# Ranks of r and c: one masked diagonal compare, and keys as columns from TensorE transposes

## The chip, the cores and the metric

One core of a Trainium2 chip. The metric is the device time of one execution in microseconds (us); lower is better.

## The reference

Two graph layers over 2708 nodes with 128 features, each followed by a residual and a layer norm. The first is a normalised diffusion plus softmax attention. The second is the one that the ranks serve:

```
XW = X @ W
s_col = XW @ a[0, :f];   s_row = XW @ a[0, f:]
Z1 = leaky_relu(s_row[:, None] + s_col[None, :], 0.01)
den = exp(Z1);  num = A @ den
att = where(num != 0, den / num, 0)
H = A @ (att @ XW)
```

The kernel calls `s_row` r and `s_col` c. It sorts the nodes by r and by c, so that for most pairs the sign of r + c (and with it the branch of the leaky relu) is known by tile, and the exponential splits into a product. For this it needs the rank of each r among all r, and of each c among all c.

## The kernel before, in words

The nodes are tiled in 22 tiles of 128 (the last has 20). Every engine has its own program; they meet at semaphores. Around the change five things run in one loop of 22 turns, one a tile `it`:

- TensorE (PE): `spread(it)`, 22 matmuls of the adjacency with the features of layer 0 (L1402); in every second turn the row transposes of a pair of tiles (L1415), in the others the products of a pair: r and c as rows over all partitions (L1425, into PSUM bank 7) and X W (L1429); then, from turn 7, `col_sums` of the rank steps of tile `it - 7`, one matmul of one column for each block (L1444).
- VectorE (DVE): the tail of tile `it` (L1030, L1033, and the two norm instructions L896, L898), then `rank_steps` of tile `it - 5`, for r (kind 0) and c (kind 1).
- ScalarE (ACT): the copies of the products (x1T L577, r and c into `rcb` L582, X W L587), then `row_sum` of the two steps of tile `it - 6` (L597).
- GpSimd (POOL): the layer norm of tile `it` (L415, L417, L423).
- SyncE: X W of each pair to DRAM.

After the loop come the rank steps of tiles 17 to 21: those of r, then (1, 17), (1, 18); then `settle(0)` turns r's ranks into positions, and steps (1, 19), (1, 20), (1, 21) stand between the works that follow it; then `settle(1)`.

A rank counts for each key the smaller ones. A step (kind, t) compares the 128 keys of tile t, as a column of per-partition scalars, with the keys of all tiles up to t, which lie as rows in `rcb`. In the version before it has three passes. First L920 takes the column out of the row: row times identity, summed over the row by the accumulator. Then L933 compares the blocks left of the diagonal with the column (`is_le`) into one of three wide buffers `Cb` (bf16), and L936 makes (equal) times the strict triangle mask U for the diagonal block. Last L942 adds (less) to that and sums it by rows with the accumulator. The wide buffer is summed by rows on ACT (`row_sum`, t blocks) and by columns on PE (`col_sums`, t blocks): a pair of different tiles is compared once and counted for both, as "less" on one side and as "not less" on the other. `settle` adds the row counts, the diagonal counts (`racc[kind][:, 1, :]`), the column sums and a constant `baseN`. A wide buffer is free for step n when the row sum and the column sums of step n - 3 are done. `Waiting` leaves out a wait that its engine has already met.

Of the kernel before, what the change touches and what calls it, by code (L numbers as in the profile page):

```python
# [5 lines left out]
P = 128  # L6
N = 2708
T = 22
# [75 lines left out]
def adj_resnorm2_kernel(nc, x, adjT, alpha, beta, W, a, rowk, out):  # L84
    with ExitStack() as ctx:
# [3 lines left out]
        def sem(name):  # L89
# [37 lines left out]
        tie = RF[:, 1664:1792].bitcast(BF16).rearrange("p (q j) -> p q j", q=2)  # L127
        junk = RF[:, 1792:1920].bitcast(BF16).rearrange("p (q j) -> p q j", q=2)
        racc = [RF[:, 1920 + 2 * T * q:1920 + 2 * T * (q + 1)].rearrange("p (q t) -> p q t", q=2) for q in range(2)]
# [75 lines left out]
        base = sq  # L205
# [31 lines left out]
        s_gset, s_rkset, s_ext, s_tie, s_less, s_diag, s_rowsum, s_rkmm, s_idx3, s_idxc = (  # L237
            sem(n) for n in ("s_gset", "s_rkset", "s_ext", "s_tie", "s_less", "s_diag", "s_rowsum", "s_rkmm",
                             "s_idx3", "s_idxc"))
# [44 lines left out]
        def less_no(n):  # L284

            return sum(t > 0 for _, t in STEPS[:n])
# [214 lines left out]
        def _(eng):  # L501
# [68 lines left out]
            def xw_part(part, g):  # L570
                t0, nb = PAIR[g]
                w, h = nb * P, g % 2
                if part == "rows":
                    av.wait_ge(s_x1T, g + 1)
                    if g >= 2:
                        av.wait_ge(s_xw, g - 1)
                    S.activation(x1T[h][:, 0:w], PSALL[:, 4, 0:w], ACT.Copy).then_inc(s_x1Tc, 1)  # L577
                else:
                    av.wait_ge(s_rc, g + 1)
                    av.wait_ge(s_xp, 12)  # L580
                    av.wait_ge(s_aoT, 6)
                    S.activation(rcb[:, :, t0 * P:t0 * P + w], PSALL[:, 7, :].rearrange("p (q n) -> p q n", q=2),  # L582
                                 ACT.Copy).then_inc(s_rcE, 1)
                    av.wait_ge(s_xw, g + 1)
                    if g >= 2:
                        av.wait_ge(s_XWd[h], 16 * (g // 2))
                    S.activation(XWb[h], PSALL[:, 4, 256:256 + w], ACT.Copy).then_inc(s_xwc, 1)  # L587

            def row_sum(kind, t):

                if t == 0:
                    return
                rows, m = rows_of(t), less_no(STEP[kind, t])
                av.wait_ge(s_less, m + 1)
# [27 lines left out]
            av.wait_ge(s_rkmm, less_no(len(STEPS)))  # L622
# [86 lines left out]
        def _(eng):  # L709
# [202 lines left out]
            def rank_steps(steps):  # L912

                for kind, t in steps:
                    n, rows, lo = STEP[kind, t], rows_of(t), t * P
                    dv.wait_ge(s_rcE, t // 2 + 1)
                    dv.wait_ge(s_const, CONST)
                    if n >= 2:
                        dv.wait_ge(s_ext, n - 1)
                    V.scalar_tensor_tensor(junk[:, n % 2, :], KEY[kind][0][:, lo:lo + P], 1.0, ident[:, :], ALU.mult,  # L920
                                           ALU.mult, accum_out=KEY[kind][1][:, t:t + 1]).then_inc(s_ext, 1)
                for kind, t in steps:
                    n, rows, lo = STEP[kind, t], rows_of(t), t * P
                    key, m = KEY[kind][0], less_no(STEP[kind, t])
                    sc1 = KEY[kind][1][0:rows, t:t + 1]
                    dv.wait_ge(s_ext, n + 1)
                    if t:
                        if m >= 3:
                            dv.wait_ge(s_rkmm, m - 2)
                            dv.wait_ge(s_rowsum, m - 2)  # L930
                        else:
                            dv.wait_ge(s_rsum, 1)
                        V.tensor_scalar(Cb[m % 3][0:rows, 0:lo], key[0:rows, 0:lo], sc1, None, ALU.is_le).then_inc(s_less, 1)  # L933
                    if n >= 2:
                        dv.wait_ge(s_diag, n - 1)
                    V.scalar_tensor_tensor(tie[0:rows, n % 2, 0:rows], key[0:rows, lo:lo + rows], sc1, U[0:rows, 0:rows],  # L936
                                           ALU.is_equal, ALU.mult).then_inc(s_tie, 1)
                for kind, t in steps:
                    n, rows, lo = STEP[kind, t], rows_of(t), t * P
                    dv.wait_ge(s_tie, n + 1)  # L940
                    dv.wait_ge(s_rkset, 2)
                    V.scalar_tensor_tensor(tie[0:rows, n % 2, 0:rows], KEY[kind][0][0:rows, lo:lo + rows],  # L942
                                           KEY[kind][1][0:rows, t:t + 1], tie[0:rows, n % 2, 0:rows], ALU.is_lt, ALU.add,
                                           accum_out=racc[kind][0:rows, 1, t:t + 1]).then_inc(s_diag, 1)

            def settle(kind):

                n = STEP[kind, T - 1]
                rank, x_, y_, hi_, lo_ = racc[kind][:, 0, :], wk[:, 0, :], wk[:, 1, :], wk[:, 2, :], wk[:, 3, :]
                dv.wait_ge(s_rkmm, less_no(n) + 1)  # L950
                dv.wait_ge(s_rowsum, less_no(n) + 1)
                dv.wait_ge(s_diag, n + 1)
                dv.wait_ge(s_dve2, base_ok)
                k1 = own.step(V.tensor_tensor(rank, rank, racc[kind][:, 1, :], ALU.add))
# [348 lines left out]
        def _(eng):  # L1303
# [102 lines left out]
            def xw_part(part, g):  # L1406
# [10 lines left out]
                else:  # L1417
                    pe.wait_ge(s_x1Tc, g + 1)
                    pe.wait_ge(s_wE, 3)
                    if g:  # L1420
                        pe.wait_ge(s_rcE, g)
                    else:
                        pe.wait_ge(s_ao, 11)
# [7 lines left out]
                    ins.then_inc(s_xw, 1)  # L1431

            def col_sums(kind, t):

                if t == 0:
                    return
                rows, m = rows_of(t), less_no(STEP[kind, t])
                pe.wait_ge(s_less, m + 1)
                if t == 1:
# [3 lines left out]
                for b in range(t):  # L1443
                    ins = TE.matmul(PSALL[:, 5 + kind, b:b + 1], Cb[m % 3][0:rows, b * P:(b + 1) * P],  # L1444
                                    ones[0:rows, :], start=False, stop=(t == T - 1 and b == t - 1))
# [238 lines left out]
```

## Time and profile before

| | |
|---|---|
| median of 3 runs | 751.45 us (749.09 to 752.02) |
| the profiled execution | 755.11 us, span 753.3 us |
| PE matmul busy | 629.9 us (84%), 4290 instructions |
| DVE busy | 598.8 us (79%), 1235 instructions |
| ACT busy | 449.8 us (60%), 693 instructions |
| POOL busy | 433.1 us (57%), 475 instructions |
| mean granted TensorE clock | 0.936 |

The loop with the ranks spans about 254 to 349 us of it, the steps of the last tiles up to about 395. Matmul records overlap, so that a duration there is longer than the step from one matmul to the next; where it matters the step is taken. In the timeline the number after x is how many instructions a row merges; "idle before" is how long the engine stood, and on what.

### The profile page before, as it was taken

The page shows a single profiled execution, that of the slowest core. Times are in us where ns is not written, and L with a number is a line of the kernel's source. Part 1 is how long each engine was busy: PE and PEld are TensorE (multiplying, and loading weights), DVE is VectorE, ACT ScalarE, POOL GpSimd, SP SyncE. Part 2 cuts the span into 40 slices and gives each one's busy share as a digit, 9 for nine tenths or more (in the row PEclk, how much of TensorE's full clock was granted, in tenths as well). Part 3 has the DMA queues.
Part 4 walks back from the last instruction along what each step waited for, and adds up shares of the span by engine and source line. Part 5 has one row for each costly group of instructions (what it writes and reads, how often), then busy time and mean ns, then how long its engine had stood idle before and what let it go on. Part 6 is the DMA issues. An engine that isn't in the chain of part 4 may idle for free.

```text
span 753.3 us, 12410 instructions
## 1 busy us (share of the span) xinstructions
PE 629.9 (84%) x4290; PEld 359.1 (48%) x4290; DVE 598.8 (79%) x1235; ACT 449.8 (60%) x693; POOL 433.1 (57%) x475
## 2 busy tenths in 40 slices
PE   5499999999996979986259879898999889886993
PEld 5243333333332969875235434444444444445882
DVE  2599999999998858999988578777788778786442
ACT  2388888888885504677840667666667667641000
POOL 5368888877777035776103257557588665201763
PEclk9999999999997689997559999999999999997997
DMA  9954444670000000000000234334334443200110
GB/s 143 103 58 40 38 41 40 148 289 1 1 1 4 2 8 22 16 15 16 7 1 19 74 85 126 98 105 121 88 101 120 122 115 91 84 4 2 31 29 16
DMA packets 19608, 45.65 MB, mean 61 GB/s; under 512 B 2922, under 2 KB 8574, under 8 KB 19486
## 3 DMA queue, kind: packets, MB, share of 16 engines
q0 software_dynamic: 9152, 31.95, 22.6%
q1 hardware_dynamic: 10334, 11.97, 4.9%
q8 instruction: 89, 1.46, 0.8%
q14 instruction: 33, 0.27, 0.1%
HBM read 56.34 MB, written 10.45 MB: 89 GB/s over the span
## 4 chain that ended last, share of the span: by engine, by line
PE 37%; DVE 30%; issue 16%; POOL 11%; ACT 3%; DMA 1%; DVEq 1%; POOLq 0%; ACTq 0%; SPq 0%
DVE ring L820 8%; PE PSALL L1636 7%; DVE R L829 7%; PE PSALL L1586 7%; POOL AW L454 6%; PE PSALL L1621 5%; PE PSALL L1402 4%; PE PSALL L1508 3%; PE PSALL L1383 2%; PE PSALL L1333 2%; DVE R L933 2%; PE PSALL L1588 2%; POOL X L445 1%; ACT XN L597 1%; PE PSALL L1457 1%
## 5 line engine op out<-in xcount | busy, mean ns | idle before, releaser
L392 POOL TENSOR_TENSOR R<-R,ring 128x452 f32<-128x452 f32 (+1 forms) x126 | 151.7, 1205 | 33.2 <-ACT ring L526 31.6
L454 POOL DMA_INDIRECT AW<-ATd,FR x66 | 90.3, 1367 | 79.0 <-DVE FR L1151 65.3
L829 DVE SCALAR_TENSOR_TENSOR R<-ring,R 128x452 bf16<-128x452 f32 (+1 forms) x132 | 134.8, 1022 | 0.0
L1586 PE MATMUL PSALL<-AW,R 128*128 128x452 fp8e4 (+1 forms) x540 | 124.3, 353 | 3.7 <-DVE R L1177 2.0
L1383 PE MATMUL PSALL<-R,AO 128*128 128x452 bf16 (+2 forms) x396 | 99.6, 361 | 16.1 <-DVE R L829 15.1
L526 ACT ACTIVATE ring<-ring,sm 128x452 f32<-128x452 f32 (+1 forms) x132 | 88.7, 672 | 27.5 <-DVE ring L820 20.9
L1333 PE MATMUL PSALL<-XN 128*128 128x452 f16 (+2 forms) x396 | 99.1, 361 | 4.7 <-issue 4.2
L534 ACT ACTIVATE R<-ring,sm 128x452 bf16<-128x452 f32 (+1 forms) x132 | 88.9, 673 | 4.3
L820 DVE TENSOR_TENSOR ring<-PSALL,AT 128x452 f32<-128x452 f32 (+1 forms) x132 | 81.0, 614 | 0.9 <-PE PSALL L1333 0.9
L1586 PEld LDWEIGHTS PSALL<-AW,R 128*128 128x128 bf16 x540 | 52.1, 97 | 56.4 <-issue 5.0
L1621 PE MATMUL PSALL<-ring,X 128*128 128x452 bf16 (+1 forms) x300 | 68.4, 362 | 12.6 <-issue 7.0
L690 ACT ACTIVATE TL<-PSALL,sm 128x452 f32<-128x452 f32 x66 | 42.0, 638 | 38.6 <-PE PSALL L1588 38.6
L1383 PEld LDWEIGHTS PSALL<-R,AO 128*128 128x128 bf16 (+1 forms) x396 | 28.4, 97 | 76.4 <-DVE R L829 62.5
L690 ACT ACTIVATE R<-PSALL,sm 128x452 f32<-128x452 f32 x66 | 42.1, 639 | 36.5 <-PE PSALL L1588 35.0
L1402 PE MATMUL PSALL<-R,AT 128*128 128x256 f16 x484 | 61.6, 288 | 0.0
L1243 DVE TENSOR_TENSOR ring<-ring 128x904 bf16<-128x904 f32 (+1 forms) x50 | 61.6, 1232 | 0.0
L1236 DVE SCALAR_TENSOR_TENSOR ring<-R,st,TL 128x904 f32<-128x904 f32 (+1 forms) x33 | 38.2, 1158 | 27.1 <-ACT TL L690 26.3
L1333 PEld LDWEIGHTS PSALL<-XN 128*128 128x128 f16 (+1 forms) x396 | 33.0, 97 | 51.7 <-DVE ring L820 28.5
L1636 PE MATMUL PSALL<-R,AT 128*128 128x256 f16 x484 | 55.3, 279 | 2.0 <-DVE R L1283 2.0
L445 POOL DMA_INDIRECT X<-XWd,idx x22 | 27.2, 1238 | 47.9 <-DVE idx L1017 41.7
L1636 PEld LDWEIGHTS PSALL<-R,AT 128*128 128x128 fp8e4 x484 | 48.4, 100 | 8.7 <-DVE R L1283 2.1
L1402 PEld LDWEIGHTS PSALL<-R,AT 128*128 128x128 fp8e4 x484 | 49.0, 103 | 7.5
(261 smaller groups left out, 1076.3 us busy)
## 6 DMA issues: line engine op xcount, KB each, us to landing
AT<-in_adjT POOLq DMA_DIRECT2D x22, 338.5 KB, 6.6
ATd<-AT SPq DMA_DIRECT2D x2, 3723.5 KB, 17.3
XWd<-ring SPq DMA_DIRECT2D x11, 128.0 KB, 1.8
out<-ring SPq DMA_DIRECT2D x21, 64.0 KB, 1.5
AW<-ATd,FR POOLq DMA_INDIRECT x66
X<-XWd,idx POOLq DMA_INDIRECT x22, 3.6
Wt<-in_W SPq DMA_DIRECT2D x1, 64.0 KB, 11.0
X<-in_x SPq DMA_DIRECT2D x1, 0.5 KB, 7.9
```

The costliest lines, as they stand in the source:

```text
L392: i = G.tensor_tensor(ES_, ES_, z, ALU.add)
L454: G.indirect_dma_start(out=AW2[:, jt % 3, q, :], out_offset=None, in_=ATd, in_offset=bass.IndirectOffsetOnAxis(ap=idxw[:, jt, q:q + 1], ax ...
L526: S.activation(z, z, ACT.Exp, scale=bcol[0:rows, :]).then_inc(s_exp, 1)
L534: S.activation(fh, z, ACT.Identity, bias=mone[0:rows, :]).then_inc(s_exp, 1)
L820: V.tensor_tensor(z, PSALL[0:rows, b, 0:w], A_, ALU.mult).then_inc(s_z, 1)
L829: V.scalar_tensor_tensor(F[0:rows, RW:RW + w], z, 1.0, F[0:rows, 0:w], ALU.subtract, ALU.subtract).then_inc(s_low, 1)
L1333: m = TE.matmul(PSALL[0:rows, b, 0:w], lh[:, jt * P:jt * P + rows], rh[:, c0:c0 + w], start=(k == 0), stop=(k == 2))
L1383: m = TE.matmul(PSALL[:, c, 0:w], half_[0:rows, jt, :], F[0:rows, o:o + w], start=(jt == 0 and k == 0), stop=(jt == T - 1 and k == 2))
L1402: ins = TE.matmul(PSALL[:, it % 4, 0:2 * D], AT[:, jt, it * P:(it + 1) * P], xp[:, jt, :, :].rearrange("p c d -> p (c d)"), start=(jt == 0 ...
L1586: TE.matmul(PSALL[:, b, 0:w], den_h[:, s + q, :, part], AW[:, jt % 3, q, c0:c0 + w], start=(q == 0 and part == 1), stop=False)
L1621: m = TE.matmul(PSALL[:, c, 0:CH[c][1]], XWh[:, jt, :, part], att[:, part_of], start=(jt == 0 and k == 0), stop=(jt == T - 1 and k == 2))
L1636: return TE.matmul(PSALL[:, out_bank[it], 0:2 * D], AT[:, jt, it * P:(it + 1) * P], xpY[:, jt, :, :].rearrange("p c d -> p (c d)"), start= ...
```

## The change

The diagonal block is written into the wide buffer beside the blocks left of it, as (`is_le`) times the mask U, by one instruction; L920, L936 and L942 with their buffers and semaphores go. Row sums and column sums take t + 1 blocks, also for t = 0. The diagonal is so counted as the other blocks are: its entries below the diagonal are compared once and serve both sides. `baseN` is changed to fit, and `settle` has no addition for the diagonal. The keys come as columns from TensorE: after the products of a pair PE waits for the copy of r and c (`s_rcE`), transposes four rows of one partition into columns of bank 7, and ACT copies them to `st` (`s_key`), before it goes on. The products of the next pair wait for `s_key` where they waited for `s_rcE`.

```diff
@@ setup (DVE) @@
-            k = own.step(V.tensor_copy(base, idx[:, 3, :]))
+            own.step(V.tensor_copy(base, idx[:, 3, :]))
             own.step(V.tensor_copy(pcol, idx[:, 0, 0:1]))
+            k = own.step(V.tensor_copy(baseN, idx[:, 0, :]))
             dv.wait_ge(s_dve2, k)
-            k = own.step(V.tensor_scalar(baseN, base, -1.0, float(N - P), ALU.mult, ALU.add))
-            dv.wait_ge(s_dve2, k)
-            k = own.step(V.tensor_copy(baseN[:, T - 1:T], idx[:, 0, T - 1:T]))
-            dv.wait_ge(s_dve2, k)
-            base_ok = own.step(V.memset(baseN[0:LAST, T - 1:T], 0.0))
+            own.step(V.tensor_scalar(baseN[:, 0:T - 1], baseN[:, 0:T - 1], -1.0, float(N - 1), ALU.mult, ALU.add))
+            base_ok = own.step(V.tensor_scalar(baseN[0:LAST, T - 1:T], baseN[0:LAST, T - 1:T], -1.0, float(N - 1),
+                                               ALU.mult, ALU.add))
@@ rank_steps (DVE) @@
                 for kind, t in steps:
                     n, rows, lo = STEP[kind, t], rows_of(t), t * P
+                    key, sc1 = KEY[kind][0], KEY[kind][1][0:rows, t:t + 1]
                     dv.wait_ge(s_rcE, t // 2 + 1)
+                    dv.wait_ge(s_key, t // 2 + 1)
                     dv.wait_ge(s_const, CONST)
-                    ... (L918 to L944: the three passes)
+                    if n >= 3:
+                        dv.wait_ge(s_rkmm, n - 2)
+                        dv.wait_ge(s_rowsum, n - 2)
+                    else:
+                        dv.wait_ge(s_rsum, 1)
                     if t:
+                        V.tensor_scalar(Cb[n % 3][0:rows, 0:lo], key[0:rows, 0:lo], sc1, None, ALU.is_le).then_inc(s_less, 1)
+                    V.scalar_tensor_tensor(Cb[n % 3][0:rows, lo:lo + P], key[0:rows, lo:lo + P], sc1, U[0:rows, :],
+                                           ALU.is_le, ALU.mult).then_inc(s_less, 1)
@@ settle (DVE) @@
-                k1 = own.step(V.tensor_tensor(rank, rank, racc[kind][:, 1, :], ALU.add))
@@ xw_part, products (ACT) @@
                     S.activation(XWb[h], PSALL[:, 4, 256:256 + w], ACT.Copy).then_inc(s_xwc, 1)
+                    av.wait_ge(s_keyT, g + 1)
+                    S.activation(st[:, 7:9, t0:t0 + nb], PSALL[:, 7, 0:2 * nb].rearrange("p (q t) -> p q t", q=2),
+                                 ACT.Copy).then_inc(s_key, 1)
@@ row_sum (ACT) @@
-                if t == 0:
-                    return
-                S.activation(Cb[3][0:rows, 0:t * P], Cb[m % 3][0:rows, 0:t * P], ACT.Copy,
-                             accum_out=racc[kind][0:rows, 0, t:t + 1]).then_inc(s_rowsum, 1)
+                S.activation(Cb[3][0:rows, 0:(t + 1) * P], Cb[m % 3][0:rows, 0:(t + 1) * P], ACT.Copy,
+                             accum_out=racc[kind][0:rows, t:t + 1]).then_inc(s_rowsum, 1)
@@ xw_part, products (PE) @@
                     if g:
-                        pe.wait_ge(s_rcE, g)
+                        pe.wait_ge(s_key, g)
                     ...
                     ins.then_inc(s_xw, 1)
+                    pe.wait_ge(s_rcE, g + 1)
+                    for kind in range(2):
+                        for q in range(nb):
+                            at = (1 - kind) * nb + q
+                            ins = TE.transpose(PSALL[:, 7, at:at + 1], rcb[0:1, kind, (t0 + q) * P:(t0 + q + 1) * P], ident[0:1, 0:1])
+                    ins.then_inc(s_keyT, 1)
@@ col_sums (PE) @@
-                for b in range(t):
+                for b in range(t + 1):
                     ins = TE.matmul(PSALL[:, 5 + kind, b:b + 1], Cb[m % 3][0:rows, b * P:(b + 1) * P],
```

## Rows read from the trace of the kernel before

**Rows 1.** The chain of waits from 240 to 400 us: start us, us, what

```profile
300.50 0.22 PE PSALL L1415 x2
...
300.91 0.36 DVE ring L920 x3
...
370.59 0.18 DVE ring L954
...
378.79 0.22 DVE ring L920 x2
379.04 1.49 DVE R L933
```

**Rows 2.** Busy us of each engine by stretch (PE, PEld, DVE, ACT, POOL), clock, DMA

```profile
290.00:305.00 15.00, 15.00 (x150) 13.52 (x149) 13.01 (x61) 8.38 (x24) 7.59 (x11) 1.00 0.07 20
...
320.00:335.00 15.00, 12.18 (x171) 10.71 (x170) 14.58 (x57) 11.37 (x20) 10.10 (x11) 1.00 0.07 19
```

**Rows 3.** The timeline of DVE, one turn: start us, duration us, instruction

```profile
316.60 0.26 DVE L920 SCALAR_TENSOR_TENSOR ring<-R,ident 128x128 bf16<-128x128 f32 x1
...
317.03 0.81 DVE L933 TENSOR_SCALAR R<-R,st 128x1152 bf16<-128x1152 f32 x1
317.76 0.34 DVE L936 SCALAR_TENSOR_TENSOR ring<-R,st,U 128x128 bf16<-128x128 f32 x1
318.02 0.81 DVE L933 TENSOR_SCALAR XN<-R,st 128x1152 bf16<-128x1152 f32 x1
...
319.01 0.34 DVE L942 SCALAR_TENSOR_TENSOR ring<-R,st,ring 128x128 bf16<-128x128 f32 x1
...
319.66 0.34 DVE L1030 SCALAR_TENSOR_TENSOR ring<-PSALL,st,AO 128x128 f32<-128x128 f32 x1
...
320.85 0.26 DVE L920 SCALAR_TENSOR_TENSOR ring<-R,ident 128x128 bf16<-128x128 f32 x1
```

**Rows 4.** The timeline of PE: products of five pairs, one set of column sums

```profile
283.24 1.03 PE L1425 MATMUL PSALL<-ring 128*128 128x256 f32 x4
...
289.57 1.03 PE L1425 MATMUL PSALL<-ring 128*128 128x256 f32 x4
...
303.16 1.03 PE L1425 MATMUL PSALL<-ring 128*128 128x256 f32 x4
...
327.57 1.03 PE L1425 MATMUL PSALL<-ring 128*128 128x256 f32 x4
...
339.83 0.79 PE L1444 MATMUL PSALL<-ones,R 128*128 128x1 bf16 x26
...
355.28 2.07 PE L1425 MATMUL PSALL<-ring 128*128 128x256 f32 x4 [0.73 <-ACT ring L577]
```

**Rows 5.** The timeline of ACT: a copy of r and c, row sums

```profile
329.59 0.58 ACT L582 ACTIVATE R<-PSALL 128x512 f32<-128x512 f32 x1
...
340.82 1.70 ACT L597 ACTIVATE XN<-XN 128x1792 bf16<-128x1792 bf16 x1 [0.36 <-DVE XN L933]
...
370.59 2.02 ACT L597 ACTIVATE XN<-R 128x2176 bf16<-128x2176 bf16 x1
```

**Rows 6.** ACT's groups from 329.5 to 370.6 us: busy, mean ns | idle before

```profile
L597 ACT ACTIVATE XN<-R 128x1664 bf16<-128x1664 bf16 (+9 forms) x12 | 22.2, 1850 | 4.2 <-DVE R L933 3.4
L597 ACT ACTIVATE XN<-XN 128x1536 bf16<-128x1536 bf16 (+4 forms) x5 | 9.3, 1868 | 0.6 <-DVE XN L933 0.4
```

**Rows 7.** Two lines' instructions: a small copy on ACT, PE's row transposes (ns min/median/max)

```profile
L509 ACT ACTIVATE sm<-PSALL x1: 173/173/173, 18.4 to 18.4; 128x1 f32<-128x1 f32 x1
...
L1415 PE MATMUL PSALL<-ident,AO x22: 272/273/477, 271.4 to 354.1; 128*128 128x128 f32 x22
```

**Rows 8.** The timelines of PE, ACT and DVE ahead of settle(1)

```profile
390.19 4.02 PE L1508 MATMUL PSALL<-AT,FR 128*84 128x452 fp8e4 x12 [2.56 <-DVE FR L1079]
...
392.10 2.44 ACT L597 ACTIVATE XN<-XN 20x2688 bf16<-20x2688 bf16 x1 [2.76 <-DVE XN L933]
...
394.90 0.18 DVE L954 TENSOR_TENSOR ring<-ring 128x22 f32<-128x22 f32 x1 [2.42 <-PE PSALL L1444]
```

More of the change, by code:

```diff
@@ L126, in adj_resnorm2_kernel @@
         Wrep, WTs = RF[:, 1280:1536], RF[:, 1536:1664]
-        tie = RF[:, 1664:1792].bitcast(BF16).rearrange("p (q j) -> p q j", q=2)
-        junk = RF[:, 1792:1920].bitcast(BF16).rearrange("p (q j) -> p q j", q=2)
-        racc = [RF[:, 1920 + 2 * T * q:1920 + 2 * T * (q + 1)].rearrange("p (q t) -> p q t", q=2) for q in range(2)]
+        racc = [RF[:, 1920 + T * q:1920 + T * (q + 1)] for q in range(2)]
         wk = RF[:, 2008:2008 + 6 * T].rearrange("p (q t) -> p q t", q=6)
@@ L235, in adj_resnorm2_kernel @@
             sem(n) for n in ("s_x1T", "s_x1Tc", "s_rc", "s_rcE", "s_xw", "s_xwc"))
-        s_gset, s_rkset, s_ext, s_tie, s_less, s_diag, s_rowsum, s_rkmm, s_idx3, s_idxc = (
-            sem(n) for n in ("s_gset", "s_rkset", "s_ext", "s_tie", "s_less", "s_diag", "s_rowsum", "s_rkmm",
-                             "s_idx3", "s_idxc"))
+        s_gset, s_rkset, s_keyT, s_key, s_less, s_rowsum, s_rkmm, s_idx3, s_idxc = (
+            sem(n) for n in ("s_gset", "s_rkset", "s_keyT", "s_key", "s_less", "s_rowsum", "s_rkmm", "s_idx3", "s_idxc"))
         s_vals, s_ohl, s_perm = ([sem(f"{n}{k}") for k in "rc"] for n in ("s_vals", "s_ohl", "s_perm"))
@@ L284, in less_no @@
         def less_no(n):
-            return sum(t > 0 for _, t in STEPS[:n])
+            return sum(1 + (t > 0) for _, t in STEPS[:n])
         def wide_of(v):
@@ L619, in _ @@
                 row_sum(1, t)
-            av.wait_ge(s_rkmm, less_no(len(STEPS)))
+            av.wait_ge(s_rkmm, len(STEPS))
             def table_factor(g):
@@ L922, in rank_steps @@
[L922 to L926, printed above, removed]
-                    if t:
[L928 to L944, printed above, removed]
+                    if n >= 3:
[3 more added lines that the diff above has]
+                        dv.wait_ge(s_rsum, 1)
@@ L950, in settle @@
-                dv.wait_ge(s_rkmm, less_no(n) + 1)
-                dv.wait_ge(s_rowsum, less_no(n) + 1)
-                dv.wait_ge(s_diag, n + 1)
+                rank, x_, y_, hi_, lo_ = racc[kind], wk[:, 0, :], wk[:, 1, :], wk[:, 2, :], wk[:, 3, :]
+                dv.wait_ge(s_rkmm, n + 1)
+                dv.wait_ge(s_rowsum, n + 1)
                 dv.wait_ge(s_dve2, base_ok)
-                k1 = own.step(V.tensor_tensor(rank, rank, racc[kind][:, 1, :], ALU.add))
                 k = own.step(V.scalar_tensor_tensor(x_, PSALL[:, 5 + kind, 0:T], -1.0, baseN,
@@ L1431, in xw_part @@
                     ins.then_inc(s_xw, 1)
+                    pe.wait_ge(s_rcE, g + 1)
[4 more added lines that the diff above has]
+                    ins.then_inc(s_keyT, 1)
             def col_sums(kind, t):
+                rows, m = rows_of(t), STEP[kind, t]
+                pe.wait_ge(s_less, less_no(m + 1))
                 if t == 0:
[L1436 to L1439, printed above, removed]
                     pe.wait_ge(s_rs, 2)
@@ L1442, in col_sums @@
                     TE.matmul(PSALL[:, 5 + kind, 0:T], U[0:1, :], U[0:1, 0:T], start=True, stop=False)
-                for b in range(t):
+                for b in range(t + 1):
                     ins = TE.matmul(PSALL[:, 5 + kind, b:b + 1], Cb[m % 3][0:rows, b * P:(b + 1) * P],
-                                    ones[0:rows, :], start=False, stop=(t == T - 1 and b == t - 1))
+                                    ones[0:rows, :], start=False, stop=(t == T - 1 and b == t))
                 ins.then_inc(s_rkmm, 1)
```

9 lines of the change are left out of this document (2 added, 7 removed).

## The prediction

> **What bounds the kernel now.** I read the chain of waits over the stretch 240 to 400 us first, then the busy shares of its parts, then the timelines of VectorE (DVE), TensorE (PE) and ScalarE (ACT) through it. The ranks are formed beside the first spread product. One turn of that loop has a PE part (22 matmuls of `spread`, row transposes or products every second turn, the column sums of two rank steps), a DVE part (four instructions of the tail, two rank steps) and an ACT part (two row sums, copies of the products). In the chain PE carries the time until 300.5 us; from 300.91 on the chain runs through the rank steps of DVE [rows 1]. The windows say the same: PE is busy 15.0 of 15 us between 290 and 305, and between 320 and 335 it is DVE with 14.6 while PE has 12.2 [rows 2]. Under DVE lies little room: ACT is 11.4 of 15 busy there, and from 329.59 on it waits for DVE only 4.8 us (4.2 + 0.6) in the 41.0 us until `settle(0)` at 370.59, which starts as ACT ends the row sum of (0, 21) [rows 1, 5, 6]. So DVE bounds the turns between 301 and about 330; behind that, DVE and ACT pass the lead back and forth; after 370.59 the path is DVE's alone until `settle(1)` at 394.90 [rows 8].
>
> **What goes from DVE.** In the turn at 316.60 us the two key extractions (L920 with their accumulator reads) take 317.03 - 316.60 = 0.43 us, the two triangle compares (L936) 0.26 each, and the two second passes (L942) 319.66 - 319.01 = 0.65 [rows 3]. The new diagonal compare is L936's form (128x128, bf16 from f32 and the bf16 mask) with other operations, so it is put at the same 0.26. Each pair of steps thus loses 0.43 + 0.65 = 1.08 us on DVE. A DVE turn was 320.85 - 316.60 = 4.25 us there [rows 3] and grows by 0.13 each turn (two compares, 0.067 more each); it becomes 3.2 there, below what PE needs (next part). DVE is then no longer the limit in the loop.
>
> **What is added to PE.** Two turns without column sums take 289.57 - 283.24 = 6.33 us [rows 4]. The column sums of 26 blocks take 0.79 us [rows 4], 0.030 each with the end of the last one in it; taken as 0.025; each step now has one block more, in all 0.05 a turn. New per pair of turns, after the products: PE waits until ACT has copied r and c (0.58 us [rows 5], begun when the products for r and c end; the XW products beside it hide about 0.4), so 0.25 with the handover; then four f32 transposes of one row. Nothing in the trace is a transpose with one moving column. Lower bound: the pitch of a one-column bf16 matmul, 0.025, so 0.1 for four. Upper bound within a stream: two 128-column f32 transposes have 0.22 us between them in the chain [rows 1], 0.11 each, 0.44 for four. I take 0.44, the same operation in the same type. So X = 0.25 + 0.44 = 0.69 us a group, with 0.35 as the low end; at the low clock (below) twice 0.44.
>
> The Trainium skill ("TensorE: Matmul & The Clock Gate", Part 4: PE-mode transpose) gives about 275 ns for a transpose in a kernel's context. The trace agrees for the duration of one (0.27 [rows 7]) and not for two back to back (0.22 [rows 1]). Were the four to cost the page's figure one after another, X would be an estimated 1.35; that is one of the rivals, priced from rows below.
>
> **Where the loop arrives.** Product group 4 starts at 303.16 now [rows 4]. PE was the limit up to there, so the four groups before it delay it by 4 x 0.69, less 0.2 of waiting on DVE that goes: 305.7. From there a pair of turns on PE is 6.33 + 0.69 + 0.025 x (blocks), with 26, 34 and 42 blocks in the next three pairs: 7.7, 7.9, 8.1. Group 7 starts at 329.4 against 327.57 now [rows 4]: 1.8 us later. DVE's 1.08 a turn is spent on the new work of PE. But today ACT is busy when group 7's product is ready and copies it only at 329.59 [rows 5]; in the changed kernel it can at 329.4 + 0.9 = 330.3. That is +0.7 at this point.
>
> **ACT from there to `settle(0)`.** Now 41.0 us. Terms: the 4.8 us of waiting for DVE go (DVE is ahead by more than a turn's slack; each step's compare needs only the row sum three steps before). A row sum covers one block more: (2.02 - 1.70)/3 = 0.107 us each [rows 5], 15 of them, +1.6. Four key copies of 128x4 from PSUM: the nearest row is the 128x1 copy with 0.17 us [rows 7]; taken as 0.25 with its gap, +1.0. ACT waits for the transposes before each: 0.1 for the handovers and 4 x 0.11, with some 0.15 for the last one to drain (a transpose's duration is 0.27 against its pitch of 0.11 [rows 1, 7]), after the copy of r and c, less the XW copy that lies in it: about 0.4; with the low clock that PE has at the last two groups (a pair of products there takes 2.07 us against 1.03 [rows 4]) about 0.8 each: +2.4 in all. Sum: -4.8 + 1.6 + 1.0 + 2.4 = +0.2. `settle(0)` comes 0.7 + 0.2 = 0.9 us later, at 371.5.
>
> The wait for the keys stands in three queues. On ACT the row sums are behind it (that is the +2.4). On PE the column sums and the next spread are behind it (that is X). On DVE `s_key` is met a turn before it is asked for, except at the last group, where step (0, 20) waits for it; ACT still has three row sums ahead of that one, about 7 us, which hide it.
>
> **From `settle(0)` to the end.** Three single steps, (1, 19), (1, 20), (1, 21), are on DVE's path. The first two lose the extraction, 379.04 - 378.79 = 0.25, and the second pass, 0.3 [rows 1, 3]: -1.1 us. Step (1, 21) ended just before 394.90 on PE (12 block sums from 390.19, waiting on DVE, then the column sum) and at 394.6 to 394.8 on ACT (392.10 + 2.44 and the accumulator's read); both come 1.1 earlier, ACT's row sum starting 0.27 later behind the diagonal compare but 0.25 earlier without the extraction [rows 8]. The first addition of each `settle` goes, 2 x 0.1. Together -1.3. Behind `settle(1)` nothing is edited. The setup's edit is one 22-column instruction less ahead of the loop, put at nothing.
>
> **Sum.** +0.9 - 1.3 = -0.4 us on the profiled execution, 755.11 to 754.7 (span 753.3 to 752.9). The median of the runs shown is 751.45, 3.7 lower, so the forecast is 751.0.
>
> Bounds: with X at 0.35, group 7 is 2.4 earlier, ACT's part 1.2 shorter: -4.0, 747.5. With ACT's waits half as long again, +1.2.
>
> **Rivals.**
> (a) DVE's saving reaches the end. For it: DVE has 14.6 of 15 us where it bounds [rows 2], and ten turns from 301 to 348 lose 1.08 each, the last ten steps 0.55 each. It needs the new work on PE near nothing and ACT with room. Against it: ACT has only 4.8 us to give after 329.6. Time: X = 0.1, key copies hidden: -0.6 x 7 at group 7, then -2.4 - 1.3 beside: about -8, 743.5. Chance 0.15 for this and all that ends below 747.7.
> (b) The round trip PE - ACT - PE costs more than its parts (slower). PE now stops after each pair of products until ACT has copied r and c. If ACT is inside a row sum then (1.2 to 2 us each), PE stands for the rest of it, and later so does the spread. ACT's two turns (about 2.0 of copies and four row sums of 0.5 + 0.107 t us each: 1.70 and the read for 14 blocks now [rows 5], and a block more) pass PE's 8.1 at t = 9 or 10; from this point PE waits for ACT. If the lag begins at group 4 instead, half a row sum (0.7) is lost at each of six groups, +4.2, and the delays return on ACT: 751.0 + 4.2 + 1.5 = 756.7. Chance 0.11.
> (c) The transposes don't pipeline: each takes the 0.27 that one lasts [rows 7] instead of 0.11, which with the 0.25 makes X = 1.35: +0.66 at seven groups before group 7's end and at four on ACT: about +7, 758. The two transposes of rows 1 with 0.22 between them speak against it; that these have one row and one column and follow a wait speaks for it. Chance 0.06.
> (d) The change does not take all it says: the diagonal compare could cost more than 0.26 as it writes into the wide buffer. At 0.34 (its duration) DVE would stay under PE; no change of the sum.
>
> **Numbers.** A measurement of this kernel tells about 0.5% (3.8 us) from no change. Forecast case, within 747.7 to 755.2: 0.68. Faster: 0.15 by (a). Slower: 0.17 by (b) and (c). The forecast's own range is 747.5 to 755; the range with the others' near halves is 745.5 to 757.5.
>
> **What would show it.** After: L920 and L942 are gone, DVE's busy time is some 24 us less (44 x 0.54), and in 320 to 335 PE is again the fuller engine with DVE waiting for `spread` before its tail. Group 4's product starts near 305.7, group 7's near 329.4, with transposes of 0.11 pitch. ACT's idle time before row sums is near nothing after 330 and it waits for the transposes by 0.4 to 0.8. `settle(0)` at about 371.5, `settle(1)` at about 394.5. It is wrong if `settle(0)` comes below 368 (then PE's added work was overpriced) or above 375 (then the round trip or the transposes were underpriced), or if something behind `settle(1)` moves.

## The result, and the profile after

| | before | after |
|---|---|---|
| median of 20 runs each | 751.68 us (748.02 to 754.8) | 755.02 us (752.11 to 759.14) |
| ratio after / before | | 1.0048 [1.003, 1.0067] |
| the profiled execution | 755.11 us, span 753.3 | 753.12 us, span 751.3 |
| mean granted TensorE clock | 0.936 | 0.939 |

The change makes the kernel 0.5% slower; I had forecast 0.4 us faster and no measurable difference. The two profiled executions say the opposite (after 2.0 us shorter): the one of before lies 3.4 us above its median, the one of after 1.9 below. So their difference may be read stage by stage where stages agree from trace to trace, but the total is the medians'. One execution of a later run (`after_level`) came in a slower state of the chip and is left out of its median.

The page's busy times of the changed kernel:

```profile
PE 633.2 (84%) x4378; PEld 362.9 (48%) x4378; DVE 577.4 (77%) x1057; ACT 456.5 (61%) x708; POOL 424.1 (56%) x475
```

DVE lost 21.4 us and 178 instructions; PE has 88 more. The chain of waits (start us, us, what) that answers to [rows 1]:

```profile
306.24 0.61 ACT R L579
...
306.90 0.40 PE PSALL L1415 x4
...
349.09 0.42 PE PSALL L1415 x4
...
367.66 1.71 ACT XN L595
...
370.40 0.19 DVE ring L934
```

The chain now goes through ACT's copy of r and c and the transposes behind it: the round trip is on the path. The same two windows as [rows 2]:

```profile
290.00:305.00 15.00, 14.51 (x148) 12.89 (x146) 9.63 (x32) 8.65 (x24) 7.31 (x13) 1.00 0.07 20
...
320.00:335.00 15.00, 14.51 (x197) 13.06 (x195) 12.02 (x29) 13.35 (x22) 8.36 (x11) 1.00 0.07 19
```

In the second window PE is the fuller engine (14.51), DVE fell from 14.58 to 12.02, ACT rose from 11.37 to 13.35. DVE's timeline of one turn (start, duration, instruction), which answers to [rows 3]:

```profile
317.48 0.81 DVE L923 TENSOR_SCALAR R<-R,st 128x1152 bf16<-128x1152 f32 x1
318.20 0.34 DVE L924 SCALAR_TENSOR_TENSOR R<-R,st,U 128x128 bf16<-128x128 f32 x1
318.46 0.81 DVE L923 TENSOR_SCALAR R<-R,st 128x1152 bf16<-128x1152 f32 x1
319.19 0.35 DVE L924 SCALAR_TENSOR_TENSOR R<-R,st,U 128x128 bf16<-128x128 f32 x1
319.45 0.35 DVE L1009 SCALAR_TENSOR_TENSOR ring<-PSALL,st,AO 128x128 f32<-128x128 f32 x1
...
323.35 0.89 DVE L923 TENSOR_SCALAR R<-R,st 128x1280 bf16<-128x1280 f32 x1 [1.47 <-PE PSALL L1427]
...
370.40 0.18 DVE L934 SCALAR_TENSOR_TENSOR ring<-PSALL,st 128x22 f32<-128x22 f32 x1 [1.05 <-PE PSALL L1427]
...
393.96 0.18 DVE L934 SCALAR_TENSOR_TENSOR ring<-PSALL,st 128x22 f32<-128x22 f32 x1 [3.71 <-PE PSALL L1427]
```

The masked compare takes 318.46 - 318.20 = 0.26 us as forecast. Every second turn DVE waits 1 to 2 us for column sums, since the three wide buffers come free at PE's pace; that wait was not forecast. Up to group 7 it costs next to nothing: PE stands only its usual 0.24 us at that group's transposes (330.71). Behind that the chain of waits runs mostly through ACT's row sums. `settle(0)` and `settle(1)` start at 370.40 and 393.96. PE, with its waits in brackets, beside [rows 4]:

```profile
305.18 1.03 PE L1404 MATMUL PSALL<-ring 128*128 128x256 f32 x4
...
306.90 0.40 PE L1415 MATMUL PSALL<-ident,R 1*128 1x1 f32 x4 [0.24 <-ACT R L579]
307.23 0.30 PE L1427 MATMUL PSALL<-ones,R 128*128 128x1 bf16 x6
...
328.99 1.03 PE L1404 MATMUL PSALL<-ring 128*128 128x256 f32 x4
...
349.09 0.41 PE L1415 MATMUL PSALL<-ident,R 1*128 1x1 f32 x4 [3.24 <-ACT R L579]
...
430.96 0.92 PE L1548 MATMUL PSALL<-R,ring 84*128 84x452 f32 x2
...
684.33 15.92 PE L1619 MATMUL PSALL<-R,AT 128*128 128x256 f16 x130 [2.03 <-DVE R L1262]
```

Four transposes occupy PE 307.23 - 306.90 = 0.33 us: with the 0.24 of waiting, X is 0.57 (forecast 0.69). ACT copies r and c at 330.06 and the keys at 331.14 (0.18 us, after a wait of 0.21). Two marks in the rows above serve from here on. The *table entry* is the first `84x452` f32 matmul, where the stage of the attention tables starts (430.96; in before 432.64), and the *output product* is the first `128x256 f16` matmul (684.33; before 685.58). Between them lies the gather stage, which the change does not touch: POOL fetches rows there by indirect DMAs, at indices that DVE prepares, and PE multiplies them.

### The profile page after: what moved, and what is told of

Its sections match the earlier page's. It is cut to its first block, busy times and chain, and to the rows that moved or that the text cites. A ratio compares the mean times of both kernels' runs of the same rounds, so it can differ in the third digit from the quotient of the medians.

```text
span 751.3 us, 12436 instructions
## 1 busy us (share of the span) xinstructions
PE 633.2 (84%) x4378; PEld 362.9 (48%) x4378; DVE 577.4 (77%) x1057; ACT 456.5 (61%) x708; POOL 424.1 (56%) x475
## 4 chain that ended last, share of the span: by engine, by line
PE 35%; DVE 26%; issue 17%; POOL 12%; ACT 6%; DMA 1%; DVEq 1%; POOLq 0%; ACTq 0%; SPq 0%
DVE ring L818 8%; PE PSALL L1619 7%; DVE R L827 7%; POOL AW L451 7%; PE PSALL L1569 5%; PE PSALL L1381 5%; PE PSALL L1604 4%; ACT XN L595 3%; PE PSALL L1491 2%; PE PSALL L1362 2%; PE PSALL L1312 2%; POOL X L442 2%; POOL X L464 1%; PE PSALL L1571 1%; PE PSALL L1440 1%
## 5 line engine op out<-in xcount | busy, mean ns | idle before, releaser
L1569 PE MATMUL PSALL<-AW,R 128*128 128x452 fp8e4 (+1 forms) x540 | 127.1, 358 | 5.5 <-DVE R L1156 2.0
L1381 PE MATMUL PSALL<-R,AT 128*128 128x256 f16 x484 | 59.4, 281 | 0.0
L1619 PE MATMUL PSALL<-R,AT 128*128 128x256 f16 x484 | 54.6, 277 | 2.0 <-DVE R L1262 2.0
L677 ACT ACTIVATE ring<-ring,st 128x904 f32<-128x904 f32 (+1 forms) x50 | 52.0, 1040 | 0.3 <-DVE ring L1215 0.3
L1619 PEld LDWEIGHTS PSALL<-R,AT 128*128 128x128 fp8e4 x484 | 48.1, 100 | 8.3 <-DVE R L1262 2.1
```

Source lines behind the costliest of these rows:

```text
L1381: ins = TE.matmul(PSALL[:, it % 4, 0:2 * D], AT[:, jt, it * P:(it + 1) * P], xp[:, jt, :, :].rearrange("p c d -> p (c d)"), start=(jt == 0 ...
L1569: TE.matmul(PSALL[:, b, 0:w], den_h[:, s + q, :, part], AW[:, jt % 3, q, c0:c0 + w], start=(q == 0 and part == 1), stop=False)
L1619: return TE.matmul(PSALL[:, out_bank[it], 0:2 * D], AT[:, jt, it * P:(it + 1) * P], xpY[:, jt, :, :].rearrange("p c d -> p (c d)"), start= ...
```

## The experiments

Sixteen runs were made, in four groups (A to D), each group on a chip of its own beside runs of the kernel before, whose medians there are 748.69, 752.31, 752.43 and 750.97 us. The last column is what is lost behind the table entry: (median - entry) less the same of before on that chip, where the entry of before is read from the controls' traces there (the first five rows; with two on a chip, their mean). `settle(1)` is the first instruction of that block, as in [rows 8]. Times in us.

| chip, kernel | ratio [95%] | median | settle(1) | table entry | output product | behind entry |
|---|---|---|---|---|---|---|
| A before_again | 1.0000 [0.9975, 1.0026] | 748.97 | 395.51 | 433.23 | 681.36 | +0.3 |
| B pad_before | 1.0014 [0.9988, 1.0040] | 754.14 | 395.18 | 432.25 | 685.36 | +1.8 |
| C pad_one | 0.9998 [0.9976, 1.0020] | 753.20 | 395.53 | 433.25 | 682.41 | +0.8 |
| D pad_again | 1.0000 [0.9976, 1.0024] | 752.41 | 394.60 | 431.68 | 682.13 | +1.7 |
| D pe_pad | 1.0009 [0.9980, 1.0038] | 752.00 | 394.46 | 432.20 | 682.32 | +0.8 |
| B late_before | 1.0081 [1.0049, 1.0113] | 758.52 | 394.18 | 436.50 | 683.08 | +2.0 |
| result: after | 1.0048 [1.0030, 1.0067] | 755.02 | 393.96 | 430.96 | 684.33 | +5.0 |
| A after_again | 1.0020 [0.9994, 1.0045] | 749.85 | 393.54 | 431.18 | 679.81 | +3.2 |
| C after_level | 1.0033 [1.0002, 1.0064] | 755.76 | 395.22 | 434.07 | 689.96 | +2.5 |
| D after_pad | 1.0027 [1.0006, 1.0049] | 754.37 | 394.45 | 431.60 | 685.27 | +3.7 |
| A keys_only | 1.0013 [0.9986, 1.0040] | 750.13 | 393.56 | 431.28 | 680.10 | +3.4 |
| B keys_deferred | 0.9979 [0.9954, 1.0005] | 751.64 | 391.02 | 428.64 | 682.22 | +2.9 |
| B diag_wait | 0.9977 [0.9955, 1.0000] | 750.78 | 391.65 | 429.29 | 682.43 | +1.4 |
| A diag_only | 0.9926 [0.9901, 0.9950] | 743.16 | 388.00 | 424.98 | 673.41 | +2.7 |
| C diag_again | 0.9957 [0.9932, 0.9983] | 748.54 | 388.82 | 425.82 | 677.40 | +3.5 |
| D diag_pad | 0.9953 [0.9925, 0.9980] | 747.74 | 389.33 | 426.30 | 678.73 | +2.4 |
| C diag_level | 1.0048 [1.0021, 1.0075] | 755.97 | 387.72 | 433.13 | 682.73 | +3.7 |

The ratio is not exactly the quotient of the two medians (`after_pad`: 1.0027 against 1.0045). Taken from the ratios instead of the medians, the last column moves by up to 1.5 us. `settle(1)` scatters too: 394.2 to 395.5 over seven traces of the old loop, 393.5 to 395.2 over four of the changed one, 387.7 to 389.3 over four of `diag_only`.

### The halves of the change, and two repeats (chip A)

`before_again` and `after_again` are the two kernels unedited.

> The kernel before, unchanged, for a second trace and as the measure of scatter. Both theories: ratio 1.000 within 0.002, settle(1) again at 394.9 us from the span's start within 0.3. Theory A (the loss lies behind settle(1)): the stretch from settle(1) to the first output matmul (before: 394.90 to 685.58, 290.7 us) is 2 to 4 us shorter here than in the first trace, since that execution was 3.4 us above the median. Theory B (the loss lies in the rank loop of ordinary executions, and the first pair of traces was not ordinary): settle(1) itself moves by over 1 us between the two traces of this kernel.

> The changed kernel, unchanged. Both: ratio 1.003 to 1.007. Theory A (loss behind settle(1)): settle(1) again at 394.0 within 0.3, that is 0.9 before the kernel before, and the stretch from there to the first output matmul longer than in before_again by 3 to 5 us. Theory B (loss in the rank loop): settle(1) at 397 or later.

`settle(1)` of the changed kernel comes at 393.54, so its loop loses nothing, as Theory A says and Theory B denies. The rest of Theory A did not come: the ratio is 1.0020, and from `settle(1)` to the output product the changed kernel takes 286.3 us against 285.9 of `before_again`, 0.4 us longer where 3 to 5 were expected. `before_again` itself has `settle(1)` 0.6 later than the first trace and this stretch 4.8 shorter.

`diag_only` is the changed kernel with the key taken by DVE as before, without the transposes; `keys_only` has the keys from TensorE and the three-pass diagonal of before (its first pass, the extraction, aside).

```
diag_only, against the changed kernel
 DVE  +  V.scalar_tensor_tensor(junk[:, n % 2, :], KEY[kind][0][:, lo:lo + P], 1.0, ident[:, :], ALU.mult,
      +                         ALU.mult, accum_out=KEY[kind][1][:, t:t + 1]).then_inc(s_ext, 1)
      -  dv.wait_ge(s_key, t // 2 + 1)
 ACT  -  S.activation(st[:, 7:9, t0:t0 + nb], PSALL[:, 7, 0:2 * nb]..., ACT.Copy)
 PE   -  pe.wait_ge(s_rcE, g + 1) and the transposes;  s_key -> s_rcE ahead of the next products
keys_only, against the changed kernel
 DVE  -  compare (is_le) * U into Cb, t + 1 blocks summed
      +  (is_equal) * U, then (is_lt) + that with accum_out, t blocks summed
```

> Only the merged diagonal compare; the keys are still taken out of the rows by DVE with identity and accumulator, and PE has no transposes. Theory A: settle(0) 1 to 3 us earlier than before (no round trip PE-ACT-PE, DVE 0.65 less a turn, row sums 0.1 longer), settle(1) 2 to 3 us earlier; the time then depends on the stage behind, which I can't price: ratio 0.995 to 1.004. Theory B (the PE-ACT-PE trip costs the time): ratio 0.996 or less.

> Only the keys by TensorE transposes; the three-pass diagonal otherwise as before. Theory A: settle(1) within 1 us of before (DVE saves 0.43 a turn, PE loses 0.7 per two turns), ratio 0.998 to 1.006, what there is of loss lies behind settle(1). Theory B: ratio 1.005 or more, settle(1) over 2 us later.

The merged diagonal alone is faster than both kernels, 0.9926, and its `settle(1)` comes 7.5 us earlier than in `before_again`, where Theory A had 2 to 3; this ratio is Theory B's. The keys alone bring nothing measurable, 1.0013, with `settle(1)` 2.0 us earlier. The busy times of `diag_only` from 320 to 335 us, then PE's product of group 7 and the table entry, then DVE's `settle(0)` and `settle(1)`:

```profile
320.00:335.00 15.00, 15.00 (x209) 13.79 (x208) 14.65 (x45) 13.86 (x21) 11.95 (x12) 1.00 0.04 12
```

```profile
323.75 1.03 PE L1410 MATMUL PSALL<-ring 128*128 128x256 f32 x4
...
424.98 0.92 PE L1548 MATMUL PSALL<-R,ring 84*128 84x452 f32 x2
```

```profile
363.87 0.18 DVE L940 SCALAR_TENSOR_TENSOR ring<-PSALL,st 128x22 f32<-128x22 f32 x1 [1.01 <-PE PSALL L1427]
...
388.00 0.18 DVE L940 SCALAR_TENSOR_TENSOR ring<-PSALL,st 128x22 f32<-128x22 f32 x1 [3.29 <-PE PSALL L1427]
```

Group 7's product starts at 323.75, where before has 327.57 [rows 4] and the changed kernel 328.99. PE is busy 15.00 of 15 us: without the second pass DVE (14.65) is already no longer the limit, the two extractions included. Moving them to TensorE then takes 0.43 us a turn from an engine that is no longer the limit and gives 0.57 us a group (0.33 of transposes, 0.24 of waiting) to the one that is. At `settle(1)` the merged diagonal is worth 7.5, 6.7 and 5.2 us (chips A, C and D, against the controls there), and the keys take 5.5, 6.4 and 5.1 of them back.

### Which part of the keys costs (chip B)

`diag_wait` has the wait without transposes and key copies; `keys_deferred` is the changed kernel with the transposes and the key copy later in their queues.

```
diag_wait, against diag_only: PE, behind the products of a group
+  pe.wait_ge(s_rcE, g + 1)
keys_deferred, against the changed kernel: PE and ACT
-  (transposes / key copy at the end of products(g))
+  if part == "rows" and g >= 1:
+      keys_part(g - 1)          # same instructions, one turn later; 9 between the last sums, 10 behind its products
```

> The merged diagonal with keys by DVE, and in addition PE waits after each pair of products for ACT's copy of r and c, as in the change, with no transposes. Theory T1 (the waiting PE - ACT is the larger part of what the keys by TensorE cost): 3 us or more above diag_only, ratio 0.997 or more. Theory T2 (each part costs its own length: the wait is 0.24 us a group, the transposes 0.36, and PE is the limit of the loop): settle(1) 2 to 3 us later than in diag_only (388.0), ratio 0.995 to 0.997.

> The changed kernel with the transposes of a group put behind the next spread (with the next rows part) and ACT's key copy there too, so that PE never stands for ACT's copy; the transposes remain. Theory T1: nearly all comes back, settle(1) within 1.5 us of diag_only's 388.0. Theory T2: only the 0.24 us a group comes back on PE and some 0.3 of waiting on ACT a group, settle(1) at 390 to 392, ratio 0.997 to 1.000.

The wait alone moves `settle(1)` from 387.7 to 389.3 (the four traces of `diag_only`, on other chips) to 391.65: +2.3 to +3.9. The ratio is T1's; `settle(1)` does not tell T1 from T2. PE's waits for ACT in `diag_wait`, 300 to 371 us (us in total, times, longest), and where the longest is:

```profile
PE PSALL L1428 <- ACT R L580: 5.5, 6, 2.8
```

```profile
343.07 1.11 PE L1410 MATMUL PSALL<-ring 128*128 128x256 f32 x4
344.02 0.61 PE L1414 MATMUL PSALL<-Wt,ring 128*128 128x128 f32 x4
...
347.43 0.95 PE L1428 MATMUL PSALL<-ones,R 128*128 128x1 bf16 x32 [2.80 <-ACT R L580]
```

The products of group 9 end near 344.6 and PE stands until 347.43, because ACT is at row sums when r and c are ready to be copied. The changed kernel has the same list:

```profile
PE PSALL L1415 <- ACT R L579: 5.0, 6, 3.2
```

Four of these six are the usual 0.24 us; group 8 has 0.76 and group 9 3.24, where two row sums (344.45 to 348.56) stand ahead of the copy in ACT's queue. That is rival (b)'s mechanism, met in full at one group rather than six. Deferring transposes and copy leaves one wait of 2.1 us on PE for this copy, and `settle(1)` comes at 391.0 against 393.5 to 395.2, 2.5 us earlier or more (chips differ), as T2 has it. The PE and ACT time of the keys stays: the result is 0.9979, beside 0.9926, 0.9957 and 0.9953 without them.

### Does the length of the program, or the moment of entry, cost time behind the loop?

The first two traces of the changed kernel enter the gather stage 1.7 and 2.1 us earlier than before's on their chips, and yet the medians are no shorter. Two theories were put up: E, that an earlier entry meets that stage's DMA traffic and clock at a worse moment; L, that DVE's shorter instruction stream shifts when code is fetched for everything behind it. These edits test them:

```
pad_before, pad_again:  before    + 176 x V.memset(TL[:, i:i + 1], 0.0)   (DVE, under the first load)
pad_one:                before    +   1 of them
after_pad:              after     + 178 of them
diag_pad:               diag_only +  90 of them
pe_pad:                 before    + 88 x TE.matmul(PSALL[:, 7, 0:1], U, ones)   (PE, before its first work)
late_before:            before    + 3 x chained V.memset(TL[:, :], 0.0)   (128x904, DVE, behind in_order(1))
after_level:            after     + 1 of them
diag_level:             diag_only + 6 of them
```

> The kernel before with 176 one-column memsets more on DVE, put where DVE waits for the first load, so that nothing on the path moves in time but the program of DVE is as much longer as the change makes it shorter. Theory L (the time behind settle(1) depends on how long the programs are or where their instructions lie): ratio 1.003 or more or 0.997 or less. Theory S (it depends on when the stage begins, or is scatter): ratio 1.000 within 0.002, if the memsets fit before the first load lands; up to +1 us if they don't.

> The kernel before with three chained 128x904 memsets on DVE after the order of c is known (in_order(1)), where DVE leads: 1.5 to 3 us of pure delay. Theory S1 (the kernel before stands at a favourable phase of the gather stage, and any other phase costs about 3 us): ratio 1.006 to 1.009, that is the delay and 3 us. Theory S2 (phase doesn't matter): the delay alone, 1.002 to 1.004. Theory S3 (waits of the gather stage swallow part of a delay as they swallowed part of the gain): less than the delay, 1.000 to 1.002.

`pad_before` is 1.0014, no difference. `late_before` is 1.0081. DVE's first memset, PE's wait for DVE and the table entry:

```profile
404.77 0.81 DVE L1092 MEMSET TL<- 128x904 f32 x1 [0.26 <-DVE st L1009]
```

```profile
407.98 0.62 PE L1536 MATMUL PSALL<-st,ring 128*128 128x22 f32 x2 [4.41 <-DVE st L1096]
...
436.50 0.92 PE L1568 MATMUL PSALL<-R,ring 84*128 84x452 f32 x2
```

About 3.2 us of memsets moved the entry 4.2 us against `pad_before` (5.3 if counted from `settle(1)`), and the median 4.4 us. PE idled 4.4 us up to 407.98, and the granted clock was 0.69 from 406 to 410 and 0.50 from 410 to 414; over 404 to 414 it was 0.67, and 0.83 in before. So the stretch from `settle(1)` to the entry is on the path, and by the medians time lost there is lost in full. The ratio falls in S1's range only because the delay was larger than S1 took it to be: behind the entry the kernel has +2.0 beside +1.8 of `pad_before`, as S2 has it. Its median is of 7 executions, and the profiled one is the shortest of them, 6.1 us below it.

> The changed kernel with one 128x904 memset (0.8 us) on DVE after in_order(1), so that the table stage begins within 0.7 us of where it does in the kernel before (432.6). Theory E (the time of the gather stage depends on when it begins): the stage takes what it takes in the kernel before, ratio 0.999 to 1.001. Theory F (it is longer in every changed program, whenever it begins): ratio 1.003 to 1.007, what the changed kernel had and the delay.

> diag_only with six such memsets, 5 to 8 us, which takes its gain back at the entry to the same stage. Theory E: ratio 0.998 to 1.001. Theory F: ratio 1.001 to 1.006, that is diag_only's 0.9926 and the delay (0.007 to 0.010), with the same 2.5 us more behind the entry as in diag_only.

> diag_only again on another chip, to confirm the version that is faster than both: ratio 0.990 to 0.995. Its entry to the table stage again near 425.0 us. Theories E and F: no difference here; the stretch behind the entry shows whether the 2.5 us above the kernel before return.

> The kernel before with a single one-column memset more on DVE at the start, hidden under the first load. Theory E: ratio 1.000 within 0.002. Theory F: the program differs by one instruction; if any difference of program costs the gather stage its 2 to 3 us, ratio 1.002 to 1.005.

Brought to before's entry time (434.07 and 433.13 against 433.25), the two edited kernels stay 2.5 and 3.7 us longer than before behind it, with ratios in Theory F's range. Theory E, by which this loss should go, has no support in either. `diag_only`'s gain repeats on another chip, 0.9957, a little less than expected.

> The changed kernel with 178 one-column memsets on DVE under the first load, as many instructions as the change removed from DVE. Theory L (length of DVE's program, so the place of its later instructions): the stretch behind the entry is again what the kernel before has, ratio 0.996 to 0.999. Rival N (not that): ratio 1.002 to 1.006, as the changed kernel.

> diag_only with 90 such memsets, as many as it removed. Theory L: 2 to 3 us below diag_only, ratio 0.988 to 0.992. Rival N: ratio 0.992 to 0.996 as diag_only.

> The kernel before with 176 memsets more, again. Theory L: 2 us slower, ratio 1.002 or more. Rival N: ratio 1.000 within 0.002.

> The kernel before with 88 one-column bf16 matmuls more on PE under the first load (PE's program is 88 matmul records longer in the changed kernel), DVE's program untouched. If the length of PE's program matters: ratio 1.002 or more (or 0.998 or less). If not: 1.000 within 0.002.

With DVE's instruction count brought back to before's, `after_pad` keeps +3.7 and `diag_pad` +2.4; 88 more matmuls in before give +0.8. All four ratios are where Theory L does not put them, so it has no support either, for DVE or for PE.

## Why the prediction was wrong

**The loop, point by point.** Its times held, within 1.1 us in both traces.

| | forecast | after | after_again |
|---|---|---|---|
| DVE busy time | -24 us | -21.4 | |
| masked compare on DVE | 0.26 us | 0.26 | |
| X, PE's loss a group | 0.69 us | 0.57 | |
| product of group 4 | 305.7 | 305.18 | 305.82 |
| product of group 7 | 329.4 | 328.99 | 329.63 |
| copy of r and c, group 7 | 330.3 | 330.06 | 330.69 |
| `settle(0)` | 371.5 | 370.40 | 370.82 |
| `settle(1)` | 394.5 | 393.96 | 393.54 |

In the two other kernels with this loop `settle(1)` is 395.22 and 394.45, so that the gain there, 0.9 in the first pair, is 0.6 by the means of all traces (394.9 and 394.3), about what was forecast. Of DVE's -24, priced alike for all 44 steps, 2.4 us did not come; I did not follow them up. Three terms on ACT were off and nearly cancelled. Its groups from 330 to 370.4 us (busy, mean ns | idle before), beside [rows 6]:

```profile
L595 ACT ACTIVATE XN<-R 128x1664 bf16<-128x1664 bf16 (+7 forms) x11 | 21.6, 1959 | 0.9 <-DVE R L924 0.2
L595 ACT ACTIVATE XN<-XN 128x1792 bf16<-128x1792 bf16 (+4 forms) x5 | 10.3, 2060 | 0.7 <-DVE XN L924 0.4
```

Its idle time before row sums fell from 4.8 us to 1.6 and not to none; it waits 0.22 us a group for the transposes, where I put 0.4 to 0.8; and a key copy holds it 0.08 us (the next instruction starts at 331.22, the copy at 331.14), where I put 0.25. (The row sums in this part are 16, not the 15 that I counted, which is 0.1 us.) ACT's part up to `settle(0)` took 40.3 us, forecast 41.2. At the low clock of the last group (0.50 from 354 to 358 us) the four transposes do take longer, but ACT does not wait for them at all there, as its copy of X W covers them. The rows are all instructions of the transposes' line in the changed kernel (ns min/median/max), and the last group's:

```profile
L1415 PE MATMUL PSALL<-ident,R x44: 194/196/261, 277.4 to 357.4; 1*128 1x1 f32 x44
```

```profile
357.10 0.58 PE L1415 MATMUL PSALL<-ident,R 1*128 1x1 f32 x4
```

**Rivals.** (a) does not occur in the changed kernel. In `diag_only`, which lacks the new work on PE, it does: I gave it 8 us, and it has 5.2 to 7.5 at `settle(1)` and 3.2 to 5.5 in the medians. (b) is there, smaller: 3.5 us above the six handovers of 0.24, nearly all of it at group 9. By then the forecast had ACT in the lead, and its time of `settle(0)` already goes by ACT's queue. (c) fails: one transpose lasts 0.196 us, and four of them 0.40, so they follow each other at about 0.07. The Trainium skill ("TensorE: Matmul & The Clock Gate", Part 4: PE-mode transpose) gives about 275 ns for a transpose; by that X would be an estimated 1.35. This case's trace has 0.196 for one of one column, and 0.40 for four, where four times the page's figure is 1.10; the trace decides. (d) does not occur.

**The step that failed** is the one sentence "Behind `settle(1)` nothing is edited", by which the sum has no term for that part and the loop's gain was to reach the end. By the first pair of traces the changed kernel enters the gather stage 1.7 us earlier than before; by the medians it ends 3.3 us later. That is the +5.0 of the table. It is partly scatter: the same kernel gave +3.2 on chip A, where its ratio was 1.0020 with 1 inside the interval, and +2.5 and +3.7 in the two variants of it. But it is not all scatter. The eleven kernels with an edited loop stand at +1.4 to +5.0 behind the entry, their median +3.2; the six on the old loop at +0.3 to +2.0, their median about +1.3 (from the ratios instead: +1.2 to +5.3 with a median of 2.7, and -0.2 to +1.8 with a median of 0.3). A single value says little: the interval of a ratio alone is about 2 us to either side, and each entry is read from one trace. Together they point to some 2 us lost behind the entry by kernels that differ only ahead of it. The traces alone say the same less firmly: from the entry to the end of the span they take 317.6 us in the mean with the old loop (seven, 314.1 to 320.7) and 319.3 with an edited one (eleven, 315.7 to 323.4). `diag_only` shows it most plainly: its entry comes 8.3, 7.4 and (as `diag_pad`) 5.6 us earlier than before's, its median 5.5, 3.9 and 3.2.

**What stays open** is the cause of these 2 us. Making up for the entry time (`after_level`, `diag_level`) or for the length of DVE's program (`after_pad`, `diag_pad`) did not remove them, and lengthening PE's (`pe_pad`) did not bring them about. But the traces show a difference of this size within 35 us behind the entry. POOL fetches rows in batches of three indirect DMAs. The fifth batch starts 31.6 to 32.5 us behind the entry in all seven traces of the old loop (mean 32.1), and 32.3 to 35.5 in the eleven of an edited one (mean 33.9). At the output product the means are 250.1 and 251.7 us, the same distance apart. In six of the eleven (`after`, `after_level`, `after_pad`, `keys_only`, `diag_again`, `diag_pad`) the granted clock falls in these 35 us, to a mean of 0.90 to 0.95; in all traces of the old loop it stays at 1.00. These six start the fourth batch 23.1 to 25.4 us behind the entry, all twelve others 22.1 to 22.8. The 35 us in before and in the changed kernel, with one of its low stretches:

```profile
432.64:467.64 35.00, 28.64 (x131) 12.93 (x131) 27.51 (x40) 23.88 (x35) 22.03 (x28) 1.00 0.37 100
```

```profile
430.96:465.96 35.00, 30.24 (x126) 13.57 (x126) 25.71 (x38) 22.24 (x33) 22.31 (x27) 0.90 0.34 95
449.00:452.00 3.00, 3.00 (x10) 1.18 (x8) 0.96 (x1) 1.30 (x3) 2.69 (x2) 0.50 0.69 170
```

The first matmuls over gathered rows lie in the other one, here in the changed kernel and then in before. They run at the low of the two clock levels (1.2 GHz; granted 0.56 from 438 to 441 us) in the one and at the high in the other:

```profile
438.47 1.68 PE L1569 MATMUL PSALL<-AW,R 128*128 128x452 fp8e4 x4 [1.58 <-DVE R L1193]
```

```profile
440.14 0.93 PE L1586 MATMUL PSALL<-AW,R 128*128 128x452 fp8e4 x4 [1.57 <-DVE R L1214]
```

That is 0.75 us at this row, and the chain of waits runs through it and the matmuls behind it up to 442.17 us. The fourth batch then starts in before and in the changed kernel at:

```profile
455.16 1.34 POOL L454 DMA_INDIRECT AW<-ATd,FR  x1 [0.70 <-DVE FR L1151]
```

```profile
455.71 1.83 POOL L451 DMA_INDIRECT AW<-ATd,FR  x1 [0.94 <-DVE FR L1130]
```

So the 1.7 us that the changed kernel is ahead at the entry are gone 25 us later, and 2.2 us have been lost. The clock is not all of it. `after_again` and `diag_only` keep 1.00 and an early fifth batch (32.4 and 32.6), and are at +3.2 and +2.7 by the medians; `diag_wait` and `diag_level` also keep 1.00 and are late at the fifth batch (35.5 and 34.0). No run moved the clock of this stretch by itself, there is one trace of each run, and why it falls only behind an edited loop is not shown.

The rest of the stage is loose as well. From the entry to the output product the same instructions take 246.6 to 255.9 us over 18 traces. POOL's waits for DVE's row indices ahead of its indirect DMAs, 440 to 680 us (us in total, times, longest), in `late_before` and `after_level`:

```profile
POOL AW L454 <- DVE FR L1154: 43.5, 20, 6.7
```

```profile
POOL AW L451 <- DVE FR L1133: 64.6, 20, 8.1
```

These two have gather stages of 246.6 and 255.9 us; before has 53.0 and 252.9, and over the 18 traces the two numbers have a correlation of 0.78. But the mean of this wait is 52.7 us with the old loop and 52.1 with an edited one: it goes with the stage's scatter, not with the edit. Within chip A the stage took 248.1 to 248.8 in all four kernels, so that these traces show no 2 us in it, while the medians of three of them do.

**The step that I should have taken and did not** is to price the halves apart. The rows of before sufficed: in 320 to 335 us DVE was 14.6 of 15 busy and PE 12.2 [rows 2]. A pair of turns took PE some 7 us there (6.33 and the column sums [rows 4]) and DVE 2 x 4.25. Without the second passes DVE needs 7.2 and PE is as good as level; the extraction's 2 x 0.43 then buys next to nothing, while X = 0.69 stands in full against it. I summed both savings into one 1.08, saw that PE would be the limit afterwards, and let the one be "spent on the new work of PE" instead of asking what each half was worth alone. The version to keep is `diag_only`, 0.9926 and 0.9957, and 0.9953 with its memsets.

## What to carry to other kernels

When a change takes two costs from the limiting engine, remove them one at a time in the sum: after the first the engine may no longer be the limit, and the second is then worth only what it costs the others. A wait of PE for ACT costs its handover where ACT is free (0.24 us here) and all that stands ahead in ACT's queue where it is not (3.24), so put the waiting work behind other work of its engine. And a stage that isn't edited still adds its own scatter (here 9 us over 18 traces): a gain or a loss of 0.3% is settled by medians, not by a pair of profiles. Where medians and stages disagree, count from a common mark to the next few events and read the granted clock there, before looking for a cause far ahead.

## What the hardware showed that was not expected

- Four f32 transposes of one row into columns occupy PE 0.33 us at the full clock; the copy of their four columns from PSUM takes ACT 0.18 us.
- Three DVE memsets ahead of a PE wait cost 4.2 us at the table entry for some 3.2 us of their own: PE idled 4.4 us, and the granted clock was 0.69 and then 0.50 from 406 to 414 us.
- Behind an unedited mark the granted clock fell for one or two stretches of about 3 us (mean of 35 us 0.90 to 0.95) in six of eleven traces with an edited loop ahead of it, and in none of seven without; the fourth batch of fetches came 0.6 to 3 us later in those six.
- Some 2 us behind the entry that follow neither its time nor the length of a program, and only in part that clock.
